# Two graph attention passes: gathered tiles kept in a ring and copied by ScalarE, resident node blocks, sums in column halves

## The reference, cut to what matters

```python
xl = (x @ Wl).reshape(N, heads, Dh)
xr = (x @ Wr).reshape(N, heads, Dh)
e = jax.nn.leaky_relu(xl[src] + xr[dst], NEG_SLOPE)
logits = jnp.einsum('ehd,hd->eh', e, att)
m = jax.ops.segment_max(logits, dst, num_segments=n_nodes)
a = jnp.exp(logits - m[dst])
denom = jax.ops.segment_sum(a, dst, num_segments=n_nodes)
alpha = a / denom[dst]
out = jax.ops.segment_sum(alpha[:, :, None] * xl[src], dst, num_segments=n_nodes)
return out.mean(axis=1) + bias
```

## Time and profile before

| | |
|---|---|
| median of the timed runs | 4050.35 us |
| profiled execution: its span, which is its own time | 4048.7 us |
| PE busy | 3293.6 us (81%) |
| DVE busy | 2807.3 us (69%) |
| POOL busy | 2796.9 us (69%) |
| ACT busy | 1717.6 us (42%) |
| edge pass of layer 1 | 189 to about 1840 us |
| edge pass of layer 2 | 2085 to about 3490 us |

### The profile page before, as it was taken

The page is one execution under the profiler, slowest core; times in us unless marked ns, Lnnn a source line. Parts: engine busy times, 40 slices in busy tenths (PEclk is TensorE's granted clock), DMA queues, the critical chain, the costliest instruction groups (busy, mean ns, idle before and its releaser), DMA issues. The chain is left out here.

```text
span 4048.7 us, 76266 instructions
## 1 busy us (share of the span) xinstructions
PE 3293.6 (81%) x24199; PEld 2204.4 (54%) x24199; DVE 2807.3 (69%) x6887; ACT 1717.6 (42%) x3696; POOL 2796.9 (69%) x2157
## 2 busy tenths in 40 slices
PE   0399999999999999996339977777777777568986
PEld 0246666666666666674226655554455555346763
DVE  3558888888888888886537755565555555579972
ACT  3254444444444444432215433333333333147861
POOL 4488888888777777505678888888888885537630
PEclk9999999999999999986669988888888888569997
DMA  2233343343333333323114433333333332211210
GB/s 58 51 65 80 86 88 86 86 89 85 80 87 86 86 85 88 75 54 83 48 36 79 91 74 67 68 69 67 67 68 73 69 68 48 52 26 40 44 34 28
DMA packets 607173, 274.68 MB, mean 68 GB/s; under 512 B 445801, under 2 KB 568077, under 8 KB 606260
## 3 DMA queue, kind: packets, MB, share of 16 engines
q1 hardware_dynamic: 261848, 102.14, 11.7%
q0 software_dynamic: 107328, 77.78, 11.1%
q10 hardware_dynamic: 237600, 89.88, 9.1%
HBM read 161.25 MB, written 105.94 MB: 66 GB/s over the span
## 5 line engine op out<-in xcount | busy, mean ns | idle before, releaser
L901 PE MATMUL L_e_ps_z<-L_e_xT,L_w_abs 128*128 128x500 f32 x2700 | 1501.4, 642 | 0.0
L826 POOL DMA_INDIRECT L_e_xs<-in_x_dram,src_idx x880 | 1193.1, 1356 | 335.4 <-issue 261.4
L826 POOL DMA_INDIRECT L_e_xs<-x_d,src_idx x820 | 1079.7, 1317 | 253.3 <-issue 249.8
L952 PEld LDWEIGHTS L_e_ps_v<-L_e_xs,L_e_p 125*128 125x128 f32 x5400 | 860.0, 204 | 628.3 <-issue 569.6
L996 ACT ACTIVATE L_e_rl<-L_e_ps_z 128x500 f32<-128x500 f32 x1350 | 793.0, 587 | 883.0 <-PE L_e_ps_z L901 883.0
L952 PE MATMUL L_e_ps_v<-L_e_xs,L_e_p 125*128 125x65 f32 x5400 | 796.2, 274 | 11.1 <-DVE L_e_acc L1180 9.4
L1180 DVE SCALAR_TENSOR_TENSOR L_e_acc<-L_e_acc,L_e_row,L_e_ps_v 128x130 f32<-128x130 f32 (+1 forms) x1440 | 448.5, 311 | 424.1 <-PE L_e_ps_v L952 281.4
L888 PE MATMUL L_e_ps_x<-ident,L_e_xs 125*64 125x125 f32 x1800 | 288.7, 285 | 310.7 <-DMA L_e_xs<-x_d,src_idx 251.8
L989 ACT ACTIVATE L_e_xT<-L_e_ps_x 128x500 f32<-128x500 f32 x450 | 264.3, 587 | 619.3 <-PE L_e_ps_x L891 590.4
L901 PEld LDWEIGHTS L_e_ps_z<-L_e_xT,L_w_abs 128*128 128x128 f32 x2700 | 427.4, 198 | 77.8 <-issue 24.3
L1163 DVE TENSOR_TENSOR L_e_p<-L_e_ohc,L_e_ae 125x640 f32<-125x640 f32 x540 | 427.1, 818 | 0.0
(11 more groups left out here) (304 smaller groups left out, 3620.2 us busy)
## 6 DMA issues: line engine op xcount, KB each, us to landing
L_v_d<-L_e_acc ACTq DMA_DIRECT2D x225, 260.0 KB
L_e_dlb<-dloc_d SPq DMA_DIRECT2D x90, 468.8 KB, 4.9
L_v_d<-L_e_acc ACTq DMA_DIRECT2D x225, 130.0 KB
L_e_xw<-x_d SPq DMA_DIRECT2D x1800, 12.0 KB
L_e_xs<-in_x_dram,src_idx POOLq DMA_INDIRECT x900
L_e_xs<-x_d,src_idx POOLq DMA_INDIRECT x900
L_e_lim<-limits_d SPq DMA_DIRECT2D x180, 39.1 KB
L_max_d<-L_e_me SPq DMA_DIRECT2D x45, 78.1 KB
```

The lines of the kernel that those rows point to most:

```text
L826: pool.indirect_dma_start(xs[c.slot(XR)][:, n, 0:D], None, lay.x_rows, bass.IndirectOffsetOnAxis(k.src_idx[:, u:u + 1], 0)).then_inc(gath[ ...
L901: pe.matmul(ps_z[part % ZR][:, 0:QT], lay.w_abs[:, part * 128:(part + 1) * 128], xT[q][:], start=True, stop=True).then_inc(s["z_ready"], 1)
L952: ins = pe.matmul(ps_v[u // 2 % 2][:, u % 2 * VX + v * XW:u % 2 * VX + (v + 1) * XW], p[st % 3][:, u % NQ, v, :, :].rearrange("e n h -> e ...
```

## The change: what it does

- **Tile ring.** POOL gathers each of the 800 tiles once instead of each of the 900 units. The tiles go to `tiles`, a ring of TR = 64, in groups of TF = 16 (`fetch_tiles`). A group is refetched when `copied` shows that the last chunk that needs it has been copied. `tiles_there` announces a group four gathers into the next one, after a wait for its data. 32 tiles are fetched ahead of the pass in layer 1, 64 in layer 2. ScalarE then copies 125 x 64 floats per unit from the ring to `xs` at an address from a register (`copy_rows`), 4 copies per step, for the chunk after the one in work. `row_places` waits until the rows are announced (`rows_there`) and loads 20 registers. `xs` is a ring of 6 chunks in both layers.
- **Resident blocks.** `xw` holds all 98 windows, loaded once per layer by one DMA. `load_windows` goes. SP loads a list of three rows of numbers per chunk (`list_units`, `serve`). PE reads the window's place from registers that it loads once per chunk (`window_blocks`). The one-hot matmul is now 128 columns wide, writes all of the 128 partitions and comes first. The transposes then write the lower 64.
- **Sums in column halves.** Each `sums` matmul (128 weight columns) becomes two of 64 columns that write to partitions 0 to 63 and 64 to 127. Sums and projections alternate by two units.
- **Layer 2: relus summed on TensorE.** `combine` isn't called. `reduce` takes the relus of both parts with a weight matrix for each (`sign_part`), 12 matmuls in place of 8.
- **Rings and setup.** Two-deep rings of `dlb` and `lim` in layer 1, the third `p` buffer in `next_node`. Seven indirect gathers of setup go, and source indices by tile are made by eight transposes.

```diff
+def fetch_tiles(k, pool, lay, f0, f1):
+    for f in range(f0, f1):
+        if f >= RF:
+            if (f - RF) % 16 == 0:
+                copies = counts(pool, f"{lay.nm}reuse{f}_", k.reuse[0:1, f - RF:min(f + 16, f1) - RF])
+            pool.wait_ge(lay.copied, copies[(f - RF) % 16])
+            pool.sem_inc(lay.freed, 1)
+        for i in range(TF):
+            g = f * TF + i
+            pool.indirect_dma_start(lay.tiles[:, g % TR * D:(g % TR + 1) * D], None, lay.x_rows,
+                                    bass.IndirectOffsetOnAxis(k.src_tile[:, g:g + 1], 0)).then_inc(lay.gath[f % RF], 16)
+            if i == 3 and f > f0:
+                tiles_there(pool, lay, f - 1)
+    tiles_there(pool, lay, f1 - 1)
...
+def serve(k, sp, lay, c):
+    sp.wait_ge(lay.ld_w[c.slot(2)], c.uses(2) * 16)
+    sp.sem_inc(lay.listed, 1)
+    sp.wait_ge(lay.fetched_to, counts(sp, f"{lay.nm}need{c.number}_", lay.lists[c.slot(LR)][0:1, 2, CU - 1:CU])[0])
+    sp.sem_inc(lay.rows_there, 1)
...
+def row_places(act, lay, c):
+    act.wait_ge(lay.rows_there, c.val(1, 1))
+    return listed(act, lay, c, 1, (TR - 1) * D)
...
+def copy_rows(act, lay, c, places, q):
+    for n in range(q, CU, NQ):
+        ins = act.activation(lay.xs[c.slot(XR)][:, n, 0:D], lay.tiles[:, bass.ds(places[n], D)], ACT.Copy)
+    if q == NQ - 1:
+        ins.then_inc(lay.copied, 1)
...
@@ TensorE: turn, reduce, sums, body
                     for j in range(Q):
                         n = j * NQ + q
-                        pe.transpose(ps[0:D, j * T:(j + 1) * T], xs[r][:, n, 0:D], k.ident[0:T, 0:T])
+                        pe.matmul(ps[:, j * T:(j + 1) * T], xw[:, bass.ds(blocks[n], 128)],
+                                  oht[c.slot(2)][:, n * T:(n + 1) * T], start=True, stop=True)
                     for j in range(Q):
                         n = j * NQ + q
-                        ins = pe.matmul(ps[D:128, j * T:(j + 1) * T], xw[c.slot(3)][:, n, :],
-                                        oht[c.slot(2)][:, n * T:(n + 1) * T], start=True, stop=True)
+                        ins = pe.transpose(ps[0:D, j * T:(j + 1) * T], xs[r][:, n, 0:D], k.ident[0:T, 0:T])
...
+                    if lay.norm:
+                        for part in range(C):
+                            for j in range(Q):
+                                ins = pe.matmul(ps_l[32 * j:32 * j + 32, 0:T], lay.sign_part[:, part, :],
+                                                rl[(C * g + part) % NE][:, j * T:(j + 1) * T], start=False, stop=part == C - 1)
...
                     for v in range(HV):
-                        ins = pe.matmul(ps_v[u // 2 % 2][:, u % 2 * VX + v * XW:u % 2 * VX + (v + 1) * XW],
-                                        p[st % 3][:, u % NQ, v, :, :].rearrange("e n h -> e (n h)"),
-                                        xs[c.slot(XR)][:, u, :], start=True, stop=True)
+                        for half in range(2):
+                            ins = pe.matmul(ps_v[u // 2 % 2][64 * half:64 * half + 64, u % 2 * VX + v * XW:u % 2 * VX + (v + 1) * XW],
+                                            p[st % 3][:, u % NQ, v, WN // 2 * half:WN // 2 * (half + 1), :].rearrange("e n h -> e (n h)"),
+                                            xs[c.slot(XR)][:, u, :], start=True, stop=True)
...
@@ ScalarE: body
                     if c.there():
                         copy_xT(c, q)
+                    one = c.back(-1)
+                    if one.there():
+                        if q == 0:
+                            if one.after(XR):
+                                act.wait_ge(s["v_ready"], one.val(CU, CU * (1 - XR)))
+                            places[:] = row_places(act, lay, one)
+                        copy_rows(act, lay, one, places, q)
```

More of the change, by code:

```diff
@@ L305, in _ @@
                 xs.wait()
+                l3.wait()
             @block.gpsimd
@@ new lines, in tiles_there, with list_units, listed @@
+def tiles_there(pool, lay, f):
+    pool.wait_ge(lay.gath[f % RF], 16 * TF * (f // RF + 1))
+    pool.sem_inc(lay.fetched_to, 1)
+def list_units(k, sp, lay, c):
+    sp.dma_start(lay.lists[c.slot(LR)][:], bass.AP(k.unit_d.tensor, c.val(CU), [[3 * UT, 1], [UT, 3], [1, CU]])).then_inc(lay.ld_w[c.slot(2)], 16)
+def listed(eng, lay, c, row, top):
+    regs = [eng.alloc_register(f"{lay.nm}{row}_{c.number}_{n}") for n in range(CU)]
+    eng.load(regs, lay.lists[c.slot(LR)][0:1, row, :])
+    return [eng.snap(r, donate=True, min_val=0, max_val=top) for r in regs]
@@ L751, in _ @@
                                    scale=1.0 - SLOPE).then_inc(s["relu"], 1)
+                act.wait_ge(s["ones"], XR + 1)
+                places = row_places(act, lay, fixed(0))
+                for q in range(NQ):
+                    copy_rows(act, lay, fixed(0), places, q)
 def edge_pass(nc, k, lay):
-    H, C, HV, XR = lay.H, lay.C, lay.HV, lay.ring
+    H, C, HV = lay.H, lay.C, lay.HV
+    SLACK = lay.slack
     HL = H // HV
@@ L965, in body @@
                     rc, rq = lag(c, q, 3)
-                    for part in range(4):
-                        if part % (4 // C) == 0 and (c.after(1) or q >= 1) and zc.there():
-                            project(zc, zq, part // (4 // C))
+                    for half in range(2):
                         if c.after(3) and bc.there():
-                            sums(bc, bq, part)
+                            sums(bc, bq, 2 * half)
+                            sums(bc, bq, 2 * half + 1)
+                        if (c.after(1) or q >= 1) and zc.there():
+                            for part in range(C // 2 * half, C // 2 * (half + 1)):
+                                project(zc, zq, part)
+                    if q == NQ - 1 and c.back(-1).there():
+                        blocks[:] = window_blocks(c.back(-1))
                     if (c.after(1) or q >= 3) and rc.there():
@@ L980, in body @@
                             weights_out(b)
+                pe.wait_ge(lay.ld_x, 16)
+                blocks[:] = window_blocks(fixed(0))
                 chunks(pe, LAST, body)
```

250 lines of the change are left out of this document (154 added, 96 removed).

## The result

The changed kernel takes 3812.35 us (median of 4 runs, 3811.1 to 3815.54). Beside it the kernel before takes 4050.26 us (4 runs, 4049.78 to 4050.52). The ratio is 0.9419 (95% interval 0.9406 to 0.9433), 237.9 us less. The forecast was 3875 us with a range of 3785 to 4010. So the direction and the range were right, and the forecast was 63 us too slow. The profiled execution's span is 3811.0 us.

The account below looks back on a forecast made before the run. Layer 1 was taken to hang on TensorE and layer 2 on POOL's gathers. Layer 2 -106, layer 1 -67 and setup -5 make -178 us, from 4048.7 to 3871, rounded to 3875 with 1.65 for the median; range 3785 to 4010.

Parts of the forecast that it names:

- the start: Layer 1: chunk 0 waits until chunk 1's rows are announced, so first work moves from 198.5 to about 228: +30 us.
- the register load: Layer 1, once per chunk: loading 20 registers costs at most 0.87 us if they load like one; taken as 0.5.
- the forecast that the projections would give time back: Layer 1, TensorE's step: two seams fewer give back 0.1 us, with projections at 3.5 us.
- the first bullet: Layer 1 sums: column halves work side by side, 54 to 60 ns a pair, sums 1.28 us per step for 1.67.
- rival 2: Layer 1: halves run one after another, 37.8 us per chunk, +131 there, total +20: 4070 us; chance 0.12.
- the prediction's own sign: Stated condition for being wrong: a register load takes microseconds and not 0.5.
- The 225 combines that leave VectorE are worth nothing: Layer 2: taking the combines off VectorE gains nothing, since it was idle for 41% of that layer.
- The group's own work: Layer 2, POOL: 0.4 us per group of gathers for register work and semaphores, 46 groups, 18 us.
- The tail and the start of layer 2: Layer 2: two more chunks follow the last gather, +47 us; 64 gathers replace 80 before the pass, -19 us with first copies.
- rival 3: Layer 2 gains nothing: data lands late, or ring and announcements lock POOL and ScalarE into turns; 3980 us, chance 0.09.
- the rivals: Layer 1 gains nothing (3970, 0.17); halves in turn (4070, 0.12); layer 2 stays (3980, 0.09); more than forecast (3755, 0.05).

Follow-up runs that it names:

- Halves in turn: Changed kernel with both units' lower column halves first, then both upper, so neighbours use the same columns: 4179.01 us, ratio 1.0187, on the 4090 chip.
- full_sums: Changed kernel with each matmul of the sums 128 weight columns wide again, still alternating by two units: 3948.03 us, ratio 0.964, on the 4090 chip.
- before_halves: Kernel before plus only the sums in column halves side by side and the order by two units: 3987.5 us, ratio 0.9865, on the 4042 chip.

## Why the prediction was right, and where it was off

| part | predicted us | measured us |
|---|---|---|
| setup | -5 | -6 |
| layer 1: chunk | 35.4 to 33.1 | 35.4 to 33.2 |
| layer 1, whole | -67 | -68 |
| merge and tables between | 0 | -8 |
| layer 2 ahead of its first turn (VectorE's wait of the earlier trace rows) | -19 | -20 |
| layer 2: its 736 gathers | 1196 | 1150 |
| layer 2: last gather to last turn | 24 to 71 | 24 to 67.5 |
| end | 0 | -1.5 |

The direction, the range and the bounds of both layers were right. The forecast was 63 us too slow, and 46 of these are the gathers of layer 2.

**Layer 1** came out as forecast, but in part by luck. The chunks save 42 x 2.2 = 92 us, 5 less than forecast, and what is left of the -68 puts the start at +24 us and not +30 (TensorE's first long wait was 16.55 us). In the chunk two wrong terms cancelled: the steps saved 5 x 0.45 = 2.25 us and not 2.75, and the register load cost next to nothing and not 0.5. The step was 6.29 for 6.2 us: projections 3.75 and not 3.5, the one-hots 0.23 and not 0.30, sums 1.22 and not 1.28. So the forecast that the projections would give time back failed: they took 3.65 us before. The side that decided, halves side by side, was the first bullet, and rival 2's price (54 ns a pass, in turn) is close to what that order costs, 56 ns. But rival 2's 37.8 us per chunk doesn't follow from the prediction's own terms, which give 7.0 us a step and 37.3 us a chunk: no change in all, and not 20 us slower. Halves in turn took 6.87 us in a plain step, for 6.74 before.

Only part of the step is the halves' doing. At full columns and with all else in place the step is 6.46 us (1013.24 to 1019.70 in full_sums). So halves are worth 0.17 us of a step there. The other 0.28 us come with the order by two units and the one-hots. As before_halves reaches 6.26 us without touching the one-hots, the order by two units is the likely source, where the prediction gave it 0.1 us. That split is argued and not run.

**The register load** was forecast at 0.5 us and took 1.36 us on TensorE's queue and 1.25 to 2.5 us on ScalarE's. By the prediction's own sign ("if a register load takes microseconds and not 0.5") it was wrong on this. It didn't hurt all the same: TensorE has no wait of its own at its load, and ScalarE's load costs TensorE 0.62 us now and then, as at 1037.43 us. From 260 to 1700 us TensorE waited for relus 7 times, 5.9 us in all, or 0.14 us per chunk. ScalarE's copies took 246 ns for the 224 forecast and lay in the gap.

**Layer 2, the step that failed.** The prediction says "The 225 combines that leave VectorE are worth nothing, since it was idle for 41% of layer 2". The share was right and the conclusion wrong: VectorE isn't on the path there, but POOL's gathers are, and they get longer when VectorE's instructions run at their start. The trace of before held that price: of its 802 gathers from 2100 to 3400 us, the 306 with no instruction of VectorE running 0.3 us after their start have a mean of 1215 ns, and all of them 1318. The runs put it at 28 and 33 us, on the pass of 820 gathers and on that of 736. It is the larger part of the 46 us by which the gathers ran faster than forecast (1.56 us each, and not 1.60 with 0.4 per group). The group's own work was the other mis-sized term, forecast at 18 us: POOL's idle time ahead of its 800 gathers is 250 us, 0.31 us each, with 11.9 us of waits for landings in it, so a group's own work all but fits into the gap of 0.30 us that POOL has anyway.

**The tail and the start of layer 2** held (43.5 for 47, -20 for -19). So rival 3, POOL and ScalarE in lockstep, did not come true on the first chip: the ring never held POOL up in layer 2 (0.3 us). In layer 1 it did, for 105 us, which is free there. On the 4055 chip the change gives 155 us and not 238. Its layer 1 ends at 1731.3 us there, so part of the gain of layer 1 is lost to the stall, which none of the rivals had.

## What to carry to other kernels

Ask of an engine that is off the path not only whether it has time but whether it makes another's instructions longer: the mean of the bounding instruction, beside an idle and beside a busy neighbour, shows it in the trace before. Look at what ran when the instruction began, too: here it was the meeting, and not the neighbour's busy share, that counted. Narrow matmuls paid where neighbours used different column strips, and cost where they used the same. Run the unchanged kernel in every batch, for 70 us between two kernels may be the chip's. And when two mis-sized terms cancel, check each against its own row before calling the forecast right.

## What was not expected of the hardware

- Loading 20 registers from SBUF takes 1.36 us on TensorE's queue and 1.25 to 2.5 us on ScalarE's. One register on SP takes 0.43 to 0.78 us in layer 1.
- A float32 pass with 64 weight columns and 65 streamed ones takes 38 ns by turns on two column halves, and 56 ns when several in a row use the same half.
- A 125-row gather on POOL takes 1.21 us beside an idle VectorE. In the rows shown it takes 1.60 to 1.87 us and ends 1.08 to 1.10 us behind the end of the VectorE instruction that ran when it began.
- The same kernel takes 3812, 3817 and 3900 us on three chips on which the kernel before takes 4050, 4042 and 4055 us.
